# A cross-attention and FFN layer: the context handed over turned as well, its chunks split as loaded, G made per batch, and new orders in the opening

## What is computed

```
enc = layernorm(x); hq = ctx                       # per batch: 512 x 512 and 77 x 512
Sim = (enc @ w1)[:, None] + (hq @ w2)[None, :] + (enc * w3) @ hq.T + b_sim
A = softmax(Sim, axis=-1)                          # over the 77 context rows
hq_hat = A @ hq
Batt = softmax(max(Sim, axis=-1)); hc_bar = Batt @ enc
hcq = concat([enc, hq_hat, enc * hq_hat, enc * hc_bar]) @ W_qv + b_qv
x = x + hcq
y = layernorm(x)
hidden = y @ W1 + b1
q = hidden + (cos(theta) * w_real + sin(theta) * w_imag) * w_imag * sin(theta + 0.1 * hidden) * 0.1
x = x + relu(q) @ W2 + b2
```

## Time and profile before

| | us |
|---|---|
| three runs | 2010.29, 2012.16, 2007.51 |
| median of the three | 2010.29 |
| the profiled execution | 2011.95 |
| its span, first to last instruction | 2010.2 |
| PE busy in it | 1976.8 (98%) |
| DVE, ACT, POOL busy | 1353.3, 964.0, 405.4 |
| opening, until the first hidden matmul of batch 0 | 89.05 |
| mean granted clock of PE | 0.997 |

### The profile page before, as it was taken

The page is one execution under the profiler, slowest core; times in us unless marked ns, Lnnn a source line. Parts: engine busy times, 40 slices in busy tenths (PEclk is TensorE's granted clock), DMA queues, the critical chain, the costliest instruction groups (busy, mean ns, idle before and its releaser), DMA issues.

```text
span 2010.2 us, 25250 instructions
## 1 busy us (share of the span) xinstructions
PE 1976.8 (98%) x9057; PEld 1625.8 (81%) x9057; DVE 1353.3 (67%) x2406; ACT 964.0 (48%) x1669; POOL 405.4 (20%) x834
## 2 busy tenths in 40 slices
PE   6989999999999999999999999999999999999999
PEld 5767788888888888888888888888888888888887
DVE  6778776767767577676767767577675767767554
ACT  6464544636445363543636445363553636445343
POOL 0122212212122121122212122121122212121110
PEclk9999999999999999999999999999999999999999
DMA  8376856757476574756757476574756757466474
GB/s 257 121 255 224 287 160 185 235 152 229 135 217 208 156 238 131 230 168 183 232 153 230 137 216 210 153 237 131 233 171 177 238 151 231 132 199 212 136 211 124
DMA packets 143679, 386.22 MB, mean 192 GB/s; under 512 B 24995, under 2 KB 34539, under 8 KB 143556
## 3 DMA queue, kind: packets, MB, share of 16 engines
q0 software_dynamic: 83584, 304.31, 49.0%
q1 hardware_dynamic: 59828, 80.27, 12.8%
q10 hardware_dynamic: 144, 0.04, 0.0%
HBM read 343.81 MB, written 40.76 MB: 191 GB/s over the span
## 4 chain that ended last, share of the span: by engine, by line
PE 93%; DVE 2%; ACT 2%; DMA 1%; issue 1%; SPq 0%; POOL 0%; ACTq 0%; DVEq 0%
PE acc L513 17%; PE acc L515 17%; PE acc L514 17%; PE hid L513 11%; PE hid L515 11%; PE hid L514 11%; PE mis L615 3%; PE acc L521 1%; PE acc L522 1%; PE mis L521 1%; PE mis L522 1%; PE mis L515 1%; PE mis L513 1%; PE mis L514 1%; DMA w_raw<-in_L_ffn_W 1%
## 5 line engine op out<-in xcount | busy, mean ns | idle before, releaser
L513 PE MATMUL hid<-T,w1s 128*128 128x512 f32 x1024 | 404.5, 395 | 5.6 <-DVE ws L1045 3.2
L513 PE MATMUL acc<-ws,act 128*128 128x512 f32 x1024 | 403.8, 394 | 0.0
L515 PE MATMUL hid<-T,w1s 128*128 128x512 f32 x1024 | 400.5, 391 | 0.0
L514 PE MATMUL hid<-T,w1s 128*128 128x512 f32 x1024 | 400.0, 391 | 0.0
L515 PE MATMUL acc<-ws,act 128*128 128x512 f32 x1024 | 399.0, 390 | 0.0
L514 PE MATMUL acc<-ws,act 128*128 128x512 f32 x1024 | 398.9, 390 | 0.0
L868 ACT ACTIVATE ph<-hid,hbias 128x512 f32<-128x512 f32 x256 | 175.9, 687 | 448.2 <-PE hid L515 448.2
L1167 DVE TENSOR_SCALAR kk<-ph 128x512 f32<-128x512 f32 x256 | 109.0, 426 | 340.3 <-ACT ph L868 337.5
L877 ACT ACTIVATE act<-h 128x512 fp32r<-128x512 f32 x256 | 162.0, 633 | 349.5 <-DVE h L1159 328.3
L1496 POOL DMA_DIRECT2D ws<-w2x_dram x240 | 127.1, 530 | 737.8 <-PE acc L515 727.5
L1173 DVE SCALAR_TENSOR_TENSOR act<-h,act 128x512 fp32r<-128x512 f32 x256 | 176.1, 688 | 93.7 <-ACT act L877 92.4
(11 more groups left out here) (172 smaller groups left out, 2762.1 us busy)
## 6 DMA issues: line engine op xcount, KB each, us to landing
w1s<-w1x_dram POOLq DMA_DIRECT2D x240, 512.0 KB, 3.7
ws<-w2x_dram POOLq DMA_DIRECT2D x240, 512.0 KB, 4.1
ws<-wqx_dram POOLq DMA_DIRECT2D x56, 512.0 KB, 3.6
X<-in_x SPq DMA_DIRECT2D x15, 1024.0 KB, 7.1
out_x<-X SPq DMA_DIRECT2D x15, 1024.0 KB, 4.4
xin<-in_x SPq DMA_DIRECT2D x14, 1024.0 KB, 6.6
w_raw<-in_L_ffn_W SPq DMA_DIRECT2D x32, 256.0 KB, 4.6
w1x_dram<-w1s POOLq DMA_DIRECT2D x16, 512.0 KB, 3.8
```

What stands on the lines that cost most here:

```text
L513: pe.matmul(dst, w_hi, m_hi, start=start, stop=False)
L514: pe.matmul(dst, w_hi, m_lo, start=False, stop=False)
L515: mm = pe.matmul(dst, w_lo, m_hi, start=False, stop=stop)
```

## The change

- The host passes two more arrays: `ctx_turned`, the context as 128 partitions x 4 x 1232 (what PE's turns made), and `columns`, the six vectors as 128 x 72. The vectors themselves are no longer passed.
- Chunks have 128 rows (the last 80) and are loaded turned. `turn`, `turn_vectors`, `g_out`, `g_dram` and their semaphores go. ScalarE and VectorE split a chunk from where it was loaded.
- `ctx_load` reads a batch's part of `ctx_turned` in one piece, and `g_high` makes G of it in place by four activations of 77 columns before its copy, for every batch.
- The products of chunks 0 to 3 are summed in `acc`, those of 4 and 5 and the late ones in `hid`. The late ones are added in tiles 3 to 6 of batch 0.
- X of batch 0 is loaded by ACT instead of SP. In batch 0 the load of the next X stands in tile 8 instead of 6.
- Each carried-over `second` waits for its own tile; the waits at the end of a batch go.
- The orders of the opening are rewritten on all engines. The table function for `trig` stands behind the first two W1 tiles.

The core of the diff:

```diff
-    CR = 126
+    CR = 128
@@ sync
             def rows_in(k):
-                need(sp, c_tr, k - 3)
-                sp.dma_start(c_rows[k % 4][0:chunk_rows(k)], ctx_flat[bass.ds(k * CR, chunk_rows(k)), :]
-                             ).then_inc(c_raw[k % 4], 16)
+                need(sp, c_tlo, k - 3)
+                m = chunk_rows(k)
+                sp.dma_start(c_rows[k % 4][:, :, 0:m], ctx_turned[:, :, k * CR:k * CR + m]).then_inc(c_raw[k % 4], 16)
+            def g_load(n, done):
+                sp.dma_start(g_view, ctx_turned[:, :, n * J:(n + 1) * J]).then_inc(done, 16)
...
-                for t in range(RT):
-                    sp.dma_start(X[:, 0, t], x_rows[0, :, t]).then_inc(x0_in[t], 16)
                 rows_in(1)
                 rows_in(2)
+                rows_in(3)
+                g_load(0, g0_in)
...
-                    if f == 6:
-                        if first:
-                            for q in range(4):
-                                sp.wait_ge(p_late[q], 16)
+                    if f == 6 and not first:
+                        x_load(n, pn)
+                    if f == NA - 2 and first:
+                        for q in range(4):
+                            sp.wait_ge(p_late[q], 16)
                         x_load(n, pn)
@@ tensor
             def attention_first():
+                multiply(0)
+                multiply(1)
+                multiply(2)
                 pe.wait_ge(s_ident, 1)
-                turn(0)
-                turn_vectors()
-                turn(1)
-                multiply(0)
                 tr_first(0, 0)
                 tr_first(0, 1)
-                turn(2)
-                multiply(1)
+                multiply(3, range(0, 2))
                 tr_first(0, 2)
                 tr_first(0, 3)
-                turn(3)
-                multiply(2)
+                multiply(3, range(2, C))
+                multiply(4, range(0, 2))
                 sim(0, 0)
-                turn(4)
-                turn(5)
+                multiply(4, range(2, C))
                 sim_rows(0)
-                multiply(3)
+                multiply(5, range(0, 2))
                 spread_max(0)
-                multiply(4)
-                turn(6)
-                turn(7)
+                multiply(5, range(2, C))
+                multiply(6, range(0, 2))
                 prob_turn(0)
-                multiply(5)
-                turn(8)
-                turn(9)
+                multiply(6, range(2, C))
                 hq_hat(0, 0)
-                multiply(6)
-                pe.wait_ge(c_tlo, CN)
+                pe.wait_ge(c_out, 4)
                 products(0, 0, True)
...
-                if not last:
-                    for p in range(STREAM - LAG, STREAM):
-                        tile_ready(b, p)
@@ scalar
             def high_parts(k):
-                sc.wait_ge(c_tr, k + 1)
+                sc.wait_ge(c_raw[k % 4], 16 * (k // 4 + 1))
                 need(sc, c_mm, k - 3)
-                nc.scalar.copy(c_turned[k % 4][:, 0], acc[:, k % 4, 0:C * CR]).then_inc(c_thi, 1)
...
+                nc.scalar.copy(c_turned[k % 4][:, 0], c_rows[k % 4]).then_inc(c_thi, 1)
...
             def g_high(n):
...
-                nc.scalar.copy(gs[:, 0].rearrange("p (c j) -> p c j", c=C), g_source(n)).then_inc(g_hi, 1)
+                for c in range(C):
+                    nc.scalar.activation(g_view[:, c], g_view[:, c], ACT.Identity, bias=w1c[:, c:c + 1],
+                                         scale=w3c[:, c:c + 1]).then_inc(gx_done, 1)
+                sc.wait_ge(gx_done, C * (n + 1))
+                nc.scalar.copy(gs[:, 0], g_raw).then_inc(g_hi, 1)
...
             def attention_first():
-                cols_load()
+                for t in range(RT):
+                    nc.scalar.dma_start(X[:, 0, t], x_rows[0, :, t]).then_inc(x0_in[t], 16)
+                nc.scalar.dma_start(cols[:], columns).then_inc(s_cols, 16)
...
-                high_parts(4)
+                high_parts(6)
+                context_high(0)
                 exponentials(0)
@@ vector
-                    if first and f < 2:
-                        product_add(GAP + 2 * f)
-                        product_add(GAP + 2 * f + 1)
+                    if first and 3 <= f < 3 + CN - GAP:
+                        product_add(GAP + f - 3)
```

More of the change, by code:

```diff
@@ L310, in chunk_of_row @@
             return r // CR
[L312 to L321, removed]
         def ctx_loads(n):
-            return 0 if n == 0 else len(g_parts(n)) + 6
+            return 0 if n == 0 else 7
         def ctx_count(n):
             return 16 * sum(ctx_loads(m) for m in range(n + 1))
[L331 to L341, removed]
+        c_rows = [v.rearrange("p (c r) -> p c r", c=C) for v in (h2[:, 0], h2[:, 1], ph[:, 0], ph[:, 1])]
+        c_turned = [act[:, q].rearrange("p a (c r) -> p a c r", c=C) for q in range(4)]
         c_product = [X[:, 1, q] for q in range(4)]
         w1q_raw, w1q = w3_sb, T[:, 1]
[L346 to L350, removed]
+        g_view = g_raw.rearrange("p (c j) -> p c j", c=C)
         block = ctx.enter_context(nc.Block())
@@ L406, in ctx_load @@
                         sp.wait_ge(p_late[k - GAP], 16)
-                g_view = g_raw.rearrange("p (c j) -> p c j", c=C)
-                for k, off, size, at_j in g_parts(n):
-                    sp.dma_start(g_view[:, :, at_j:at_j + size], g_dram[k, :, :, off:off + size]).then_inc(ctx_in, 16)
+                g_load(n, ctx_in)
                 stack_load(n, hq_raw, hq_tail, ctx_flat, ctx_in)
@@ L586, in hidden, with second @@
                           c == 0, c == C - 1, hid_done if c == C - 1 else None)
-            def second(b, f, whole, ready=False):
+            def second(b, f, whole):
                 g = FT * b + f
@@ L592, in second @@
                 p = place_w2(f, whole)
-                if not ready:
-                    tile_ready(b, p)
+                tile_ready(b, p)
                 w = ws[:, slot_of(p)]
@@ L769, in body @@
                     elif not first:
-                        second(b - 1, FT + f - LAG, False, True)
+                        second(b - 1, FT + f - LAG, False)
                     if last:
@@ L811, in high_parts @@
             def high_parts(k):
-                sc.wait_ge(c_tr, k + 1)
+                sc.wait_ge(c_raw[k % 4], 16 * (k // 4 + 1))
                 need(sc, c_mm, k - 3)
-                nc.scalar.copy(c_turned[k % 4][:, 0], acc[:, k % 4, 0:C * CR]).then_inc(c_thi, 1)
-                sc.wait_ge(cols_done, 1)
-                need(sc, g_stored[g_slot(k)], g_stores(g_slot(k), k))
-                for c in range(C):
-                    cs = slice(c * CR, (c + 1) * CR)
-                    nc.scalar.activation(c_gfull[g_slot(k)][:, cs], acc[:, k % 4, cs], ACT.Identity,
-                                         bias=w1c[:, c:c + 1], scale=w3c[:, c:c + 1]).then_inc(c_g, 1)
+                nc.scalar.copy(c_turned[k % 4][:, 0], c_rows[k % 4]).then_inc(c_thi, 1)
             def product_copy(k):
@@ L966, in attention_first @@
                 w1_high(1)
+                sc.wait_ge(s_args, 1)
+                nc.scalar.activation(trig[:], arg[:], ACT.Sin).then_inc(s_trig, 1)
                 product_copy(7)
@@ L1579, in body @@
                         w1_store(f + 2)
-                    if first and f < 2:
-                        for k in range(GAP + 2 * f, GAP + 2 * f + 2):
-                            late_product_out(k)
+                    if first and 3 <= f < 3 + CN - GAP:
+                        late_product_out(GAP + f - 3)
                     if first:
@@ L1617 @@
         args.append(nc.dram_tensor(f"in_{name}", a.shape, _mybir.dt.from_np(a.dtype), kind="ExternalInput").ap())
+    P = 128
+    a = _np.asarray(inputs['ctx_1024'])
+    b, j, d = a.shape
+    turned = _np.ascontiguousarray(a.reshape(b * j, d // P, P).transpose(2, 1, 0))
+    w = _np.asarray(inputs['L0_xattn_w_sim']).reshape(-1)
+    parts = [inputs['L0_ffn_quantum_phases'], inputs['L0_ffn_quantum_weights_real'], inputs['L0_ffn_quantum_weights_imag'],
+             inputs['L0_ffn_b1'], w[0:d], w[2 * d:3 * d]]
+    columns = _np.ascontiguousarray(_np.concatenate([_np.asarray(v).reshape(-1, P).T for v in parts], axis=1))
+    for name, a in (("ctx_turned", turned), ("columns", columns)):
+        arrays[f"in_{name}"] = a
+        args.append(nc.dram_tensor(f"in_{name}", a.shape, _mybir.dt.from_np(a.dtype), kind="ExternalInput").ap())
     shape = inputs['x'].shape
```

210 lines of the change are left out of this document (89 added, 121 removed).

## The result

The changed kernel takes **2018.59 us** (median of 5 runs, 2017.29 to 2019.01) against 2010.29 us before (5 runs, 2007.51 to 2012.68): ratio 1.0045, 95% interval 1.0033 to 1.0057. It is 8.3 us slower; 14.6 us faster was forecast, and the range ended at 2003. The profiled execution has a span of 2016.8 us, 6.6 more than before.

A forecast was written before the change was run, and what follows sets the result against it. PE was taken as the bound, busy 1976.8 of 2010.2 us, with its idle time in the first 220 us. Terms -9.8 + 0.1 - 4.9 = -14.6 took 2010.3 to 1995.7, range 1988.5 to 2003.

The forecast's parts named there:

- Part 5: Fifteen steady batches: activations shift ScalarE's later work by 1.36, within 1.5 us of room at the similarity; 0.
- Part 3: First tile loop: activations +1.36 against a table load of 1.28 gone, +0.1; moved X load 0 (bounds -3 and +4).
- Rival C: Steady batches: activations wait for each other, shift 2.5 or more, 15 to 20 us lost, slower overall; chance 0.04.
- Part 1: Opening up to the sum over W0: PE's turns and ScalarE's G of the whole context go; -9.8 (bounds -12.5 and -6).
- Step a: Start of the opening: X and W1q share DMA; PE's steady work starts at 8.9 instead of 12.28, similarity at 26.5.
- Step b: Opening, similarity to first W0 matmul: PE idles 2.2 for the softmax and 1.4 for W0's weights; ready at 44.2.
- rival A: Opening's attention chain is later, through late hqw rows or costlier context copies; 5 later makes 2001; chance 0.16.
- Part 2: Rest of the opening, 55.68 to 89.05 before: same matmuls back to back, VectorE's new order covered by PE; 0.
- rival B: First tile loop: moved X load hits harder, 2 us and a half-clock stretch more, 1999.5; chance 0.07.
- Part 4: Edge of batch 0: PE's wait for split tiles and the half clock behind it go; -4.9 (bounds -3.2 and -5.5).
- Rival D: Edge of batch 0 gains nothing, as PE meets a late W1 or W2 tile soon after; 2000.5; chance 0.06.
- Rival E: Start: X on another queue shares DMA with W1q; X first gives 1997.3, last 1994 at best; chance 0.06.

The follow-up runs named there:

- hqw_copies_later: ctx_copies_later with ScalarE's two hqw copies and VectorE's low half of hqw moved behind the softmax's probabilities in the opening: 1997.48 us, ratio 0.9939.
- x_behind_w1: ctx_copies_later with batch 1's X load issued one step later, in tile 10 behind the W1 tile of tile 12: 1994.86 us.
- edge_waits_back: The changed kernel with PE's waits on three weight tiles put back to the end of each batch: 2023.59 us.
- ctx_copies_later: The changed kernel, all activations kept, with ScalarE's four context copies moved from tile 2 to tile 3: 1999.82 us, ratio 0.9948.
- g1_in_opening: ctx_copies_later with the activations and copy of G for batch 1 moved from tile 1 to the end of the opening: 1999.36 us.
- all_four_moves: The changed kernel with context copies in tile 3, X load behind W1 tiles, hqw copies behind the softmax, batch 1's G in the opening: 1988.90 us, ratio 0.9900.

## Why the prediction was wrong

**Part 5 failed.** Its sentence "VectorE's g_low ends at 357.35 + 0.47 = 357.8, the first weight load of the similarity is at 359.3: 1.5 us of room. 0" read the room at the first consumer of the shifted work. It was right for that consumer: the similarity waits in no steady batch. But the shift ran on, over the T copies, VectorE's low halves and `h`, relu and sine of tile 2 and four context copies, to `sim_bias`, whose room was 0.4. There PE waited 1.05 us in each batch, 14.7 in all, and the two runs that take the activations out and move the copies away both end that. That row, 364.02 against 365.10, was in the trace before. The size of the shift was nearly right: 1.36 taken (bounds 1.2 to 1.8), 1.50 measured. With 0.4 of room the step would have read 1.50 - 0.4 = 1.1 a batch. The factor of 15 was one too many: PE waits 14 times, because batch 1's similarity stands in batch 0 and belongs to Part 3. 14 x 1.1 = 15.4 would have made the sum +0.8, about no change. Measured are 14 x 1.22 = 17.1, since each wait also costs 0.17 beyond its length. In spans the parts measure -9.3, +0.8, +0.3 and +2.6 (the two terms of Part 3), -5.0 and +17.1, together +6.5 against the 6.6 by which the spans differ. The part's own rule, that each tenth beyond the room is paid in every batch, was right; what it was applied to was the wrong room.

For the size: the prediction let the row of 126 columns (1.50 for four) set 0.30 for an activation of 77 columns. Four of 77 take this (ScalarE's timeline after, opening):

```profile
13.80 1.48 ACT L773 ACTIVATE tmp_w<-tmp_w,cols 128x77 f32<-128x77 f32 x4 [0.50 <-DMA tmp_w<-in_ctx_turned]
```

The copy behind them starts at 15.31, 1.51 after the first. The Trainium skill's page "ScalarE: Activation LUTs" (Rules for kernel authors), by which the prediction estimated a shift of 1.5 to 1.6, agrees with that better than the price taken; "so the row decides" was the wrong verdict on it. It would not have saved the forecast: at the similarity even 1.5 cost nothing.

**Rival C was right in sign and wrong in mechanism.** It needed a shift of 2.5 or more, a late gs and activations that do not overlap. The shift was 1.5, gs was in time, and the groups of four overlap. Its chance of 0.04 rested on "1.5 us of room".

**Part 1** forecast -9.8 at the W0 block and got -9.3. Step a held: first product matmul 9.02 (forecast 8.9), similarity 25.7 (26.5). Step b was too short: the wait for the probabilities was 4.7, not 2.2. This is rival A in small, by the 2.71 us that ScalarE waited for the hqw rows; `hqw_copies_later` puts its worth at about 2 us. The block at 46.4 against 44.2, or 45.9 with the low clock that was counted, is what that made.

**Part 2** (0) was 0.8: PE has a wait of 0.99 us for T at 76.69, where it was 0.18 before.

**Part 3** had two terms. The activations against the table load, +0.1: the lead went from 8.5 to 8.2, so the number held, in part by luck. As forecast, the waits for T ahead of gs shrank by 1.2 (the lead is 9.7 in tile 2) and that for gs went from 3.4 to 4.9. Not forecast were a half-clock stretch behind it (1.9; the lead falls to 6.3) and the end of a wait of 1.7 for `sim_rows` behind that (the lead is 8.2 again). These two nearly cancel. The moved X load, 0 with a bound of +4: the lead fell from 8.2 to 5.5 by tile 12, so it cost 2.6 against the place it had. This is rival B's longer wait, without the further half-clock stretch: in its old place the load cost 3.7 (2.05 of waiting and the half clock), in the new one 6.4. "The same stall moves two tiles" named the place, hidden 11 straight behind hidden 10, and gave it no price. `x_behind_w1` shows that the load need not stall anything.

**Part 4** (-4.9) measured -5.0 in the trace (the lead at the second hidden tile of batch 1 is 10.6, and it was 5.5 in tile 12) and 5.0 in `edge_waits_back`. Rival D is out: PE waits for no weight tile after 200 us.

**Rival E,** whether X on ScalarE's queue shares the DMA with W1q: the quarters of W1q were used at 7.02, 8.20, 9.17 and some 9.9 us, a little before the case of sharing (last at 10.9). From issue to landing a quarter of W1q took 6.3 us (median; 4.8 before, with X behind it in the same queue) and a quarter of X 4.8 (5.7 before): W1q got slower and X faster. That speaks for sharing, and against X or W1q going first. No run moved X, so its price stays open.

The low end of the range should read 1988.3 by its own terms (1995.7 - 1.7 - 3 - 2.7), not 1988.5; nothing hangs on it.

With the loss that Part 5 missed taken out, the change is worth about 10 us: that is `ctx_copies_later`, 1999.8 against 2009.6 in its series, inside the range given.

## What to carry to other kernels

A step put early into an in-order engine's queue delays everything behind it, and idle time behind it gives the delay back only if what the engine waits for there is not delayed by the same step. Here ScalarE's 2.09 us of idling gave nothing back, because they were a wait for VectorE, which was late by the same 1.5 us. So the room to read is the smallest over all the instructions behind it that another engine waits for, and not the one at its own consumer. Where a queue is short of room, look first for work in it that is needed late, as the context copies were (tile 3, used from tile 7): moving it costs one line and gave 18.8 us, more than the whole change had been forecast to give. A small cost that repeats in every batch can outweigh what is won once in the opening; here 1.22 us in each of 14 batches outweighed a lead of 10.6.

## What the runs showed of the hardware

Narrower activations were hardly cheaper here: four of 77 columns took 1.48 us and four of 126 columns 1.50. They differ in more than width: the wider ones read `acc`, which PE writes, and the narrower ones `tmp_w`, which a DMA loads. A copy of 512 columns took 0.59 us from PE's `mis` and 0.62 from `w_sb` (both from ScalarE's timelines), so the source counts as well, and the two rows do not separate width from source.

The length of an idle stretch of PE alone does not tell the clock behind it here. After 4.86 us (97.08 after) and 4.65 us (150.82 after) matmuls started 0.43 us apart, at a granted clock of 0.50, which is the level of 1.2 GHz. After 3.36 us for gs before they started 0.23 us apart, at 2.4 GHz. After 3.2 us at the edge of batch 0 the half clock set in at the first matmul in `edge_waits_back` and after the third in the kernel before. After 3.0 us for gs it set in after the second matmul in `g1_in_opening` and not at all in `all_four_moves`.

A short wait in a full stretch cost more than it lasted: 1.05 us of idling made each batch 1.22 us longer, at a granted clock of 1.00.
